# An adaLN layer on one core: normalisation of the residual tile moved to ScalarE, two waits moved to first use

## What is computed

```python
sa, ca, ga, sb, cb, gb = mod            # six rows of 512 per sequence
h = layernorm(x) * (1 + ca) + sa
x = x + ga * attention(h)               # ends in: heads @ Wo + bo
h = layernorm(x) * (1 + cb) + sb        # layernorm: (x - m) / sqrt(v + eps)
x = x + gb * ffn(h)                     # silu(h @ Wg) * (h @ Wu) @ Wd
```

## Time and profile before

| | |
|---|---|
| median of 3 runs | 2425.92 us (2419.62 to 2426.41) |
| the profiled execution, its own time | 2425.46 us |
| its span | 2423.7 us |
| PE busy over the span | 2211.0 us (91%) |
| DVE, ACT, POOL busy | 1207.5, 790.4, 755.8 us |
| TensorE's granted clock, mean | 0.964 |
| projection stage, first DMA issue to the first load of the next stage | 1199.0 to 1363.4 us |
| DVE busy in 1230 to 1320 | 83.85 of 90 us |

### The profile page before, as it was taken

One profiled execution on the slowest core, in us unless ns is written; L12 is line 12 of the kernel. 1 busy time (PEld: TensorE's weight loads), 2 busy tenths in 40 slices (PEclk: granted clock), 3 DMA queues, 4 the chain that ended last, 5 costly groups with the idle time before them and its releaser, 6 DMA issues. The chain is left out here.

```text
span 2423.7 us, 31792 instructions
## 1 busy us (share of the span) xinstructions
PE 2211.0 (91%) x11496; PEld 1588.9 (66%) x11496; DVE 1207.5 (50%) x2775; ACT 790.4 (33%) x1671; POOL 755.8 (31%) x732
## 2 busy tenths in 40 slices
PE   6999993699899999999578799999999999999998
PEld 3777772454554554554266588888888888888887
DVE  5999995566666666665289412212122222222212
ACT  3333331155555555555345311111111111111111
POOL 2666775012212212212276122222222222222221
PEclk8999997599999999999899899999999999999999
DMA  6222223555465465452388411211121212121111
GB/s 226 70 87 104 104 87 111 121 130 134 107 151 132 108 154 128 107 137 68 84 273 298 157 32 52 70 53 65 53 70 48 70 53 70 48 66 35 53 53 52
DMA packets 164833, 243.66 MB, mean 101 GB/s; under 512 B 20605, under 2 KB 87293, under 8 KB 164185
## 3 DMA queue, kind: packets, MB, share of 16 engines
q1 hardware_dynamic: 160504, 229.27, 32.8%
q0 software_dynamic: 3136, 9.46, 1.4%
q10 hardware_dynamic: 1056, 3.15, 0.3%
HBM read 131.69 MB, written 59.26 MB: 79 GB/s over the span
## 5 line engine op out<-in xcount | busy, mean ns | idle before, releaser
L1353 DVE TENSOR_TENSOR f_gu<-f_psU,f_silu 128x512 f32<-128x512 f32 x128 | 88.6, 692 | 712.6 <-PE f_psU L1420 712.6
L990 ACT ACTIVATE b_probT<-b_psB 128x512 f32<-128x512 f32 (+3 forms) x768 | 336.0, 490 | 280.5 <-PE b_psB L849 274.7
L920 DVE TENSOR_REDUCE b_top<-b_psA 128x2 f32<-128x1024 f32 (+2 forms) x320 | 287.8, 902 | 121.5 <-PE b_psA L831 121.3
L1309 POOL TENSOR_SCALAR f_wd_hi<-f_wd 128x512 fp32r<-128x512 f32 x128 | 83.4, 652 | 820.0 <-PE f_psD L1405 776.3
L849 PE MATMUL b_psB<-b_stack 98*128 98x512 f32 (+3 forms) x768 | 253.8, 397 | 6.8 <-ACT b_probT L990 6.8
L849 PEld LDWEIGHTS b_psB<-b_stack 98*128 98x128 f32 x768 | 131.1, 189 | 171.1 <-issue 106.5
L1329 ACT ACTIVATE f_silu<-f_psG 128x512 f32<-128x512 f32 x128 | 76.7, 599 | 504.5 <-PE f_psG L1420 504.5
L786 POOL TENSOR_SCALAR_AFFINE_SELECT b_probT<-b_probT 128x512 f32<-128x512 f32 x128 | 81.1, 634 | 486.6 <-ACT b_probT L990 486.6
L831 PE MATMUL b_psA<-b_stack 96*128 96x512 f32 (+3 forms) x768 | 191.9, 370 | 43.0 <-DVE b_top L920 20.9
L1418 PE MATMUL f_psG<-f_hT_hi,w_hi 128*128 128x512 f32 x512 | 200.4, 391 | 11.2 <-DVE f_hT_lo L1347 11.2
L1419 PE MATMUL f_psG<-f_hT_hi,w_lo 128*128 128x512 f32 x512 | 200.1, 391 | 0.0
(11 more groups left out here) (173 smaller groups left out, 3985.3 us busy)
## 6 DMA issues: line engine op xcount, KB each, us to landing
b_stack<-b_halves SPq DMA_DIRECT2D x192, 256.0 KB, 4.9
f_wd<-in_wd_t SPq DMA_DIRECT2D x128, 256.0 KB, 2.7
qkv_d<-a_t SPq DMA_DIRECT2D x32, 512.0 KB, 2.7
b_land<-qkv_d SPq DMA_DIRECT2D x32, 512.0 KB, 4.3
a_x<-in_x SPq DMA_DIRECT2D x32, 256.0 KB, 3.3
qkv_d<-a_v SPq DMA_DIRECT2D x32, 256.0 KB, 3.0
b_v<-qkv_d SPq DMA_DIRECT2D x16, 512.0 KB, 5.8
att_d<-b_att SPq DMA_DIRECT2D x16, 512.0 KB, 3.4
```

The source lines that it names most:

```text
L920: last = dve.tensor_reduce(into, tile[:, :, 0:width], AX.X, ALU.max, negate=True)
L990: act.activation(probT[:, (NW * n + w) % PROBS, j, 0:width], psB[:, i % 2, 0:width], ACT.Exp).then_inc(s["expd"], 1)
```

## The change

`xh` is now made by ACT, in a new part `normal` at the end of ACT's step: `xh = rs * x1 + nm`, one activation with a column for its scale and one for its bias. DVE's `norm` keeps the reciprocal and computes the new column `nm = -mean * rs` (128x1) in place of the 128x512 operation. The semaphore `rs` now counts two per tile. DVE's write of `x1` waits, in addition, until ACT has read the buffer's last content. ACT's wait for the modulation columns moves to its first `modulate`, DVE's wait for the gates to its first `residual`.

```diff
--- before.py
+++ after.py
@@ -1043,6 +1043,7 @@
         mv = sb("p_mv", [P, 4, 2])
         sd = sb("p_sd", [P, 4])
         rs = sb("p_rs", [P, 4])
+        nm = sb("p_nm", [P, 4])
         h2 = sb("p_h2", [P, 4, KC, P])
         spots = sb("p_spots", [1, 4])
         wland = sb("p_wland", [P, 2, PIECE])
@@ -1062,6 +1063,9 @@
         def done(b, t):
             return b * TB + (t + 1)
 
+        def twice(b, t, n):
+            return b * (2 * TB) + (2 * t + n)
+
         def uses(b, t):
 
             return b * (16 * TB // 4) + 16 * (t // 4 + 1)
@@ -1137,8 +1141,15 @@
                 act.wait_ge(s["mv"], done(b, t))
                 act.activation(sd[:, t % 4:t % 4 + 1], mv[:, t % 4, 1:2], ACT.Sqrt, bias=eps[:, 0:1]).then_inc(s["sd"], 1)
 
+            def normal(b, t):
+                act.wait_ge(s["rs"], twice(b, t, 2))
+                at_least(act, s["turned"], done(b, t - 2))
+                act.activation(xh[:, t % 2], x1[:, t % 4], ACT.Identity, scale=rs[:, t % 4:t % 4 + 1],
+                               bias=nm[:, t % 4:t % 4 + 1]).then_inc(s["xh"], 1)
+
             def modulate(b, t):
-
+                if isinstance(b, int) and b == 0 and t == 0:
+                    act.wait_ge(s["mod_in"], 16 * 2 * B)
                 at_least(act, h2_out[t % 4], uses(b, t - 4))
                 pause(nc, act, spots[:, t % 2:t % 2 + 1], psT[0:1, t % 2, 0:1], s["turned"], done(b, t))
                 for k in range(KC):
@@ -1146,8 +1157,7 @@
                     last = act.activation(h2[:, t % 4, k], psT[:, t % 2, k * P:(k + 1) * P], ACT.Identity, bias=m[0], scale=m[1])
                 last.then_inc(s["h2_ready"], 1)
 
-            act.wait_ge(s["mod_in"], 16 * 2 * B)
-            stagger(act, B, TB, [(root, 3), (high, 0), (modulate, 4)])
+            stagger(act, B, TB, [(root, 3), (high, 0), (modulate, 4), (normal, 3)])
 
         @block.vector
         def _(dve):
@@ -1170,11 +1180,14 @@
                 dve.tensor_tensor(at_lo[:, t % 2], at[:, t % 4], at_hi[:, t % 2].bitcast(F32), ALU.subtract).then_inc(s["at_lo"], 1)
 
             def residual(b, t):
+                if isinstance(b, int) and b == 0 and t == 0:
+                    dve.wait_ge(s["gate_in"], 16 * B)
                 dve.wait_ge(s["projected"], done(b, t))
                 g = gate[:].rearrange("p b n -> p (b n)")[:, bass.ds(b * DM, DM)]
                 dve.tensor_tensor(gated[:, t % 2], psP[:, t % 2], g, ALU.mult).then_inc(s["gated"], 1)
                 dve.wait_ge(x_in[t % 4], uses(b, t))
                 at_least(dve, x1_out[t % 4], uses(b, t - 4))
+                at_least(dve, s["xh"], done(b, t - 4))
                 dve.wait_ge(s["gated"], done(b, t))
                 dve.tensor_tensor(x1[:, t % 4], gated[:, t % 2], x[:, t % 4], ALU.add).then_inc(s["x1"], 1)
                 dve.wait_ge(s["x1"], done(b, t))
@@ -1185,12 +1198,10 @@
             def norm(b, t):
                 dve.wait_ge(s["sd"], done(b, t))
                 dve.reciprocal(rs[:, t % 4:t % 4 + 1], sd[:, t % 4:t % 4 + 1]).then_inc(s["rs"], 1)
-                at_least(dve, s["turned"], done(b, t - 2))
-                dve.wait_ge(s["rs"], done(b, t))
-                dve.tensor_scalar(xh[:, t % 2], x1[:, t % 4], mv[:, t % 4, 0:1], rs[:, t % 4:t % 4 + 1],
-                                  ALU.subtract, ALU.mult).then_inc(s["xh"], 1)
-
-            dve.wait_ge(s["gate_in"], 16 * B)
+                dve.wait_ge(s["rs"], twice(b, t, 1))
+                dve.scalar_tensor_tensor(out=nm[:, t % 4:t % 4 + 1], in0=mv[:, t % 4, 0:1], scalar=-1.0, in1=rs[:, t % 4:t % 4 + 1],
+                                         op0=ALU.mult, op1=ALU.mult).then_inc(s["rs"], 1)
+
             stagger(dve, B, TB, [(norm, 3), (residual, 2), (low, 0)])
 
         @block.tensor
```

## The result

| | before | changed |
|---|---|---|
| median, 7 runs each | 2423.43 us (2419.62 to 2426.41) | 2414.39 us (2410.7 to 2415.45) |
| profiled execution, span | 2423.7 us | 2413.7 us |
| projection stage, load of Wo to the next stage's first load | 164.5 us | 157.0 us |
| first matmul, from the load of Wo | 16.3 us | 10.7 us |
| first and last product with the gate, from the load of Wo | 21.0, 155.4 us | 16.1, 145.3 us |

The ratio is 0.9961, with a 95% interval of 0.995 to 0.9973. That is 9.5 us less, between 6.5 and 12.1, where 13.0 were forecast. Of the 10.0 us between the two profiled spans 7.5 lie in the stage; 2.4 us lie ahead of it, where nothing was changed, and are taken as the scatter of single executions. The stage began at 1198.96 us before and begins at 1196.55 now, so times are best compared from there.

What follows compares the result with a forecast made beforehand. DVE was taken to set the projection stage's pace, DMA close behind. From 2425.46 us, the last tile's residual starting 14.4 us earlier, less 1.4 us of tail, gave 13.0 us off: 2412.5 us; range 2402 to 2421 us.

Steps and rivals of the forecast that it cites:

- The start: Start of the projection stage: without the wait for the modulation columns, everything from PE's first matmul comes 5.6 us earlier.
- The small column: DVE's new 128x1 operation: mean near 0.4 us while POOL works, 0.15 us without it.
- the stretched and the unstretched case: DVE's 128x1 operation beside POOL: forecast inherits 0.29 us of lengthening; rival inherits none, 2408.6 us, chance 0.24.
- The pace under POOL: Projection stage while POOL loads weight pieces: a tile period of 4.12 us, down from 4.52 us.
- the stretch: DVE operations lengthened beside POOL: 0.85 us in 4.52 us, a share of 0.187 going by time, not by tile.
- The sum's own 3.35 us for DVE's step: DVE's tile period without POOL, falling from 3.71 to 3.35 us.
- Hidden with 0.6 us to spare: ACT's `normal`: `xh` is ready 2.5 us into PE's `project` of 3.14 us, so PE doesn't wait.
- the three signs by which the prediction called itself wrong: PE waits for `xh` ahead of its transposes, DVE waits for the square root, POOL's pieces take much longer than 3.5 us.
- The rival of the held loads: Late attention-tile loads hold ACT: at a 6.0 us landing, 4.45 us per tile, 2419.7 us; chance 0.12.
- PE's floor: PE's least time per tile, 3.60 us, which becomes the bound once POOL's work has ended.
- 340 GB/s: Estimated full DMA rate; with POOL's 75 GB/s it gives at least 3.96 us per tile while POOL loads.
- The tail: End of the projection stage: the last `normal` stands behind `modulate` of the tile before on ACT, costing +1.4 us.

Runs made afterwards that it cites:

- early_at: The changed kernel with the attention tile's load issued two steps earlier, the load of x left in place: 2413.9 us, ratio 0.9953.
- one_input: The changed kernel with the small column made by tensor_scalar from one tensor, in place of scalar_tensor_tensor with two: 2409.08 us, ratio 0.9933.
- one_early: The changed kernel with the small column made from one tensor and the attention tile's load issued two steps earlier: 2401.71 us, ratio 0.9902.

## Why the prediction was right, and what was mis-sized

- **The bound and the direction.** DVE set the pace, taking its 128x512 normalisation away paid, and the range held the result. The runs split the gain: 3.6 us by the waits alone, 5.6 us by the normalisation alone.
- **The start.** 5.6 us forecast, 5.7 at the first matmul. One term was missing: the first product followed 5.4 us behind that matmul instead of 4.7, since ten of the thirteen matmuls ran at the lower clock and not seven, so 5.0 us reached DVE. And by the run with the waits alone some 3.6 us of it reach the end.
- **The small column.** Forecast 0.4 us under POOL and 0.15 without; measured 0.43 and 0.16. The choice between the stretched and the unstretched case was the right one for this kernel, and the run with one input shows why. That the mean is so near to 0.4 us is luck in part: in the run with the normalisation alone it is 0.27 us.
- **`normal`.** 0.82 us forecast, 0.80 measured.
- **The pace under POOL** was forecast at 4.12 us and is 4.26. Here a term of the sum failed: the stretch was taken to go by time and to shrink with the period to 0.77 us; it stayed 0.85 us per tile (0.30 + 0.28 + 0.27). With it 0.07 us per tile of waiting for the square root (2.1 us in 28 tiles), which the sum had at nothing. The two make the 0.14 us between 4.12 and 4.26 (0.15 by their rows); over 28 periods that is 3.9 us. The sum's own 3.35 us for DVE's step was a little long: behind POOL's end products come 3.25 us apart, and the run with the early load leaves 4.09 - 0.88 = 3.21 us. So, as an estimate from these figures, 0.15 to 0.2 us of the 4.26 are waits, more than the 0.07 seen ahead of the reciprocal.
- **"Hidden with 0.6 us to spare"** for `normal` held only where `high` was on time. It often was not: ACT waited 24.1 us for loads, and PE 10.8 us for `xh`. Two of the three signs by which the prediction called itself wrong came, PE's waits for `xh` and DVE's for the square root (3.0 us); the third, much slower pieces, came in small (3.77 us each instead of 3.51). So the main term held, and the claim that `normal` costs nothing on ACT failed. The rival of the held loads had the mechanism, and priced it at a landing of 6 us as the point; 5.1 us in the median was enough for single tiles to be late, since the landings scatter from 3.0 to 12.7 us. What the loads cost is not to be added to DVE's part: lifting one bound alone uncovers the other, as early_at, one_input and one_early show. That the two alternate from tile to tile is argued from the waits.
- **POOL's end** was taken as fixed, 127 us from the stage's start; its pieces slowed (3.51 to 3.77 us each, with more waits for their loads) and it ended at 135, so more tiles ran beside it. After its end the period is 3.25 us, and PE's last two bias matmuls are 3.48 us apart (1335.05 and 1338.53), so the 3.60 us taken for PE's floor was too long.
- **340 GB/s** as the full DMA rate was too low: one_early moved 333 at a share of 0.95, which makes 351 by the same division, and a stretch of early_at shows more still, below.
- **The tail** was forecast at +1.4 us and is +2.7. I counted `normal` behind `modulate` once. But the `modulate` that it stands behind needs the `xh` of its own tile, which stood behind a `modulate` too: it ends 5.4 us after the last product (1345.81 + 1.47) and not 4.2 as in the earlier trace rows.

The last product was forecast at 141.0 us from the stage's start and came at 145.3, and the tail was 1.3 us longer, so the stage ended 5.5 us later than forecast: it gave 7.5 us of the 13.0. That the median, 2414.39 us, is only 1.9 us from 2412.5 is luck in part: the forecast was reckoned down from the profiled execution, 2425.46 us, and the median of the kernel before turned out 2.0 us below that.

## What to carry to other kernels

When an operation leaves the engine that sets the pace, look at what form the small operation that stays has: a column made from two SBUF tensors beside a busy GpSimd cost 0.27 us of stretch in the mean, nearly what the full tile had (0.11 us in another run), and the same column from one tensor none. When two bounds lie within some tenths of a microsecond of each other (here DVE's step and the loop of load, `high`, `modulate`, store, load), test edits in pairs: alone they gave 2.7 and 6.6 us of the stage, together 13.5. Here it paid to let a load wait for its own buffer alone, and not behind the stores of later parts in its queue, but only once the other bound was lifted.

## What the runs showed of the hardware

The stretch beside POOL does not shrink with the size of VectorE's operation: 128x1 with two tensors went from 159 to as much as 1058 ns, 128x1 with one tensor stayed within 212 to 215. With the product written to PSUM instead of SBUF, the product took 692 ns beside POOL (684 into SBUF) and the addition that reads it back 692 ns, what the addition from two SBUF tensors takes without POOL (693). And the DMA rate at which the queues are full is not where I took it from the earlier trace rows: a stretch of 10 us in early_at shows 379 GB/s at a share of 1.02.

```profile
1234.00:1244.00 10.00, 9.77 (x47) 7.60 (x46) 9.53 (x18) 7.81 (x21) 6.54 (x9) 1.00 1.02 379
```
